# A narrow attention layer's score matmuls in two 64-row tiles, with another order of the work in a step

## What is computed

```python
# layer 1 (narrow), x: 2048 x 256, cond: 1601 x 512
q = rmsnorm(x) @ wq           # 16 heads of 16
k, v = cond @ wk, cond @ wv   # 4 heads of 16, each for 4 query heads
x = x + softmax(q @ k.T / 4) @ v @ wo
```

## Time and profile before

| | us |
|---|---|
| median of 3 runs | 4579.02 (4578.73 to 4581.03) |
| the profiled execution | 4576.37 |
| its span | 4574.6 |
| TensorE busy | 4481.5 |
| VectorE busy | 3081.8 |
| GpSimd busy | 2825.7 |
| ScalarE busy | 2308.6 |

### The profile page before, as it was taken

One profiled execution on the slowest core, in us unless ns is written; L12 is line 12 of the kernel. 1 busy time (PEld: TensorE's weight loads), 2 busy tenths in 40 slices (PEclk: granted clock), 3 DMA queues, 4 the chain that ended last, 5 costly groups with the idle time before them and its releaser, 6 DMA issues.

```text
span 4574.6 us, 56775 instructions
## 1 busy us (share of the span) xinstructions
PE 4481.5 (98%) x20609; PEld 2828.0 (62%) x20609; DVE 3081.8 (67%) x5037; ACT 2308.6 (50%) x4121; POOL 2825.7 (62%) x1365
## 2 busy tenths in 40 slices
PE   8999999999999979999999999999999999999999
PEld 7888765656566445555556566656656666666664
DVE  4221567777777678777846777777766677777776
ACT  3232554555455436666655554545555545555553
POOL 0000388889888701011136898889875888898886
PEclk9999999999999979999999999999999999999999
DMA  5474921222221021111243222222126212222220
GB/s 189 156 221 150 305 68 38 66 66 69 48 64 48 13 41 15 13 14 16 57 133 92 64 69 47 66 64 64 41 50 219 63 45 60 63 69 61 51 48 30
DMA packets 124633, 349.68 MB, mean 76 GB/s; under 512 B 28085, under 2 KB 46005, under 8 KB 113338
## 3 DMA queue, kind: packets, MB, share of 16 engines
q1 hardware_dynamic: 124352, 346.04, 28.6%
HBM read 191.31 MB, written 120.31 MB: 68 GB/s over the span
## 4 chain that ended last, share of the span: by engine, by line
PE 93%; DVE 5%; issue 1%; DMA 1%; ACT 0%; SPq 0%; DVEq 0%; ACTq 0%
PE ST L1005 14%; PE SS L986 12%; PE ST L1006 12%; PE OA L1016 12%; PE OB L1016 11%; PE ST L1150 5%; PE OA L1158 4%; PE SS L1136 3%; DVE acc L1612 2%; PE OB L1136 1%; PE SS L1025 1%; PE ST L1081 1%; PE ST L1082 1%; PE ST L1083 1%; PE SS L1052 1%
## 5 line engine op out<-in xcount | busy, mean ns | idle before, releaser
L882 POOL TENSOR_TENSOR acc<-acc,P 128x1024 f32<-128x1024 f32 x912 | 2216.9, 2463 | 298.4 <-DVE acc L1618 285.3
L1346 ACT ACTIVATE P<-ST 128x512 f32<-128x512 f32 (+1 forms) x2496 | 1464.6, 598 | 1254.2 <-PE ST L1006 1128.6
L1591 DVE TENSOR_REDUCE mpart<-SS 128x1 f32<-128x400 f32 (+1 forms) x3072 | 1629.5, 570 | 666.4 <-PE SS L986 590.7
L1005 PE MATMUL ST<-QX,KX 128*128 128x512 f32 (+1 forms) x2496 | 1022.9, 410 | 2.3 <-ACT stw L1244 2.0
L986 PE MATMUL SS<-KS,QS 68*128 68x400 f32 (+1 forms) x3072 | 977.2, 352 | 13.6 <-DMA QS<-stq 8.0
L1006 PE MATMUL ST<-QS,KS 69*128 69x512 f32 (+1 forms) x2496 | 988.4, 396 | 0.0
L986 PEld LDWEIGHTS SS<-KS,QS 68*128 68x128 f32 x3072 | 583.6, 190 | 189.8 <-DVE xacc L1642 24.9
L1005 PEld LDWEIGHTS ST<-QX,KX 128*128 128x128 f32 (+1 forms) x2496 | 463.0, 186 | 359.5 <-issue 271.2
L1016 PE MATMUL OA<-P,Vp 128*64 128x512 f32 (+1 forms) x2496 | 658.3, 606 | 0.0
L1016 PE MATMUL OB<-P,Vp 128*64 128x512 f32 (+1 forms) x2496 | 641.3, 592 | 0.0
L1445 ACT ACTIVATE PG<-ST 128x512 f32<-128x512 f32 (+1 forms) x832 | 426.5, 616 | 215.6 <-PE ST L1150 215.5
(11 more groups left out here) (247 smaller groups left out, 4457.1 us busy)
## 6 DMA issues: line engine op xcount, KB each, us to landing
q_parts<-stq SPq DMA_DIRECT2D x96, 512.0 KB, 5.2
QX<-q_parts SPq DMA_DIRECT2D x96, 512.0 KB, 11.3
KX<-k_parts SPq DMA_DIRECT2D x48, 801.0 KB, 9.4
QS<-q_parts SPq DMA_DIRECT2D x45, 512.0 KB
R<-R SPq DMA_DIRECT2D x360, 64.0 KB, 2.0
v_tiles<-sv SPq DMA_DIRECT2D x24, 832.0 KB, 5.9
Vp<-v_tiles SPq DMA_DIRECT2D x24, 832.0 KB, 7.2
k_parts<-skh SPq DMA_DIRECT2D x48, 400.5 KB, 4.8
```

Source lines behind the costliest of these rows:

```text
L882: gp.tensor_tensor(out, out, P[0:k, slot(H, t), q, :], ALU.add).then_inc(pool_a, 1)
L1005: pe.matmul(bank, KX[H % 2][:, t * 128:t * 128 + k], QX[H % 2][:, q], start=True, stop=False)
L1346: act.activation(P[0:k, slot(H, t), j, :], ST[n % 3][0:k, :], ACT.Exp, scale=SCALE).then_inc(act_p, 1)
L1591: dve.tensor_reduce(mpart[H % 2][:, i // len(KCH), c:c + 1], SS[RING_AT["s", H, i] % 3][:, 0:w], AX.X, ALU.max).then_inc(dve_ss, 1)
```

## The change

The contraction of a narrow head is cut to the three products high-high, low-high and high-low: 48 rows for a maximum (`GROWS`), 49 for a score. The operands lie twice in the partitions, at 0 and at 64 (`HALF`). Of the keys both copies are the same; of the queries the first half holds blocks 0 and 2 of 512 columns, the second blocks 1 and 3. Score j of a tile reads half j % 2, maximum i half i % 2. Nothing reads partitions that must be zero any more: three memsets go, and eight of 32 rows replace four.

A head is now thirteen steps of one key tile: three scores of the next tile, the output items or the projection where there are any, five maxima (four in one step of thirteen, seven in most of head 0), the transposed row in step 9, the fourth score, then the values of this step's tile. The ring's fourth bank is OA, and the values go to OB. The query parts take six DMAs a head instead of four, the maxima row two instead of one, the key parts 24 instead of 16 in all. VectorE and ScalarE follow the same order.

```diff
-MROW = 3 * QD + D1
+GROWS = 3 * D1
+HALF = 64
...
+GROW = KT - 4
...
+def group_units(h, t):
+
+    if t + 1 < KT:
+        return [(0, t + 1, j) for j in range(JQ)]
+    return [(1, 0, j) for j in range(JQ)] if h + 1 < HEADS else []
+
+
+def group_tiles(h, t):
+
+    if t >= GROW:
+        return 2, (part(SUNITS, t - GROW, KT) if h + 2 < HEADS else range(0))
+    if h + 1 >= HEADS:
+        return 1, range(0)
+    return 1, (part(SUNITS, t, GROW) if h == 0 else part(SUNITS, t + KT - GROW, KT))
+
+
+def group_takes_row(h, t):
+    return t == GROW and h + 1 < HEADS
+
+
+def group_takes_sums(h, t):
+    return t == 3 and h > 0
+
+
+def group_o_items(h, t):
+
+    return range(2 * t, 2 * t + 2) if h % GROUPS == 1 and h > GROUPS and t < JQ else range(0)
+
+
+def group_q_item(h, t):
+
+    return t if h % QHEADS == QHEADS - 2 and h + 2 < HEADS and t < JQ else None
...
+        GS = SS + [OA]
...
-        GS = SS + [OB]
...
+            def group_k(g):
+                for i, r in enumerate((0, 0, 1)):
+                    for half in range(2):
+                        to = HALF * half + i * D1
+                        sp.dma_start(words(KG[g][to:to + D1, :]), dKG[r, g * QD:g * QD + D1, :]).then_inc(gd_k, 16)
...
-                stack(GQ[h % 3], words(Q4hi[q, :]), words(Q4lo[q, :]), (0, 1, 0, 1), D1, gd_q[h % 3])
+                for i, src in enumerate((Q4hi, Q4lo, Q4hi)):
+                    blocks = words(src[q, :]).rearrange("d (b u c) -> d b u c", b=2, u=2)
+                    for half in range(2):
+                        to = HALF * half + i * D1
+                        sp.dma_start(words(GQ[h % 3][to:to + D1, 0:NQ // 2]).rearrange("d (b c) -> d b c", b=2),
+                                     blocks[:, :, half, :]).then_inc(gd_q[h % 3], 16)
...
-                sp.dma_start(words(GQ[h % 3][MROW:MROW + 1, :]).rearrange("o (t p) -> o t p", p=128),
-                             words(mrow[:, :])).then_inc(gd_m, 16)
+                for half in range(2):
+                    to = HALF * half + GROWS
+                    sp.dma_start(words(GQ[h % 3][to:to + 1, 0:NQ // 2]).rearrange("o (t p) -> o t p", p=128),
+                                 words(mrow[8 * half:8 * half + 8, :])).then_inc(gd_m, 16)
...
-                    gp.memset(words(k[3 * QD:4 * QD, :]), 1.0).then_inc(pool_ones, 1)
-                gp.wait_ge(pool_ones, GROUPS)
-                for q in GQ:
-                    gp.memset(words(q[:, :]), 0.0).then_inc(pool_ones, 1)
+                    for half in range(2):
+                        gp.memset(words(k[HALF * half + QD:HALF * half + 2 * QD, :]), 1.0).then_inc(pool_ones, 1)
...
             def group_s(h, i):
-                at = GRING_AT["s", h, i]
                 if i == 0:
-                    pe.wait_ge(gd_q[h % 3], 64 * (h // 3 + 1))
-                wait_group_ring(pe, at)
-                qt, (o, w) = i // len(KCH), KCH[i % len(KCH)]
-                pe.matmul(GS[at % 4][:, 0:w], GQ[h % 3][0:MROW, qt * 128:(qt + 1) * 128],
-                          KG[h % GROUPS][0:MROW, o:o + w], start=True, stop=True).then_inc(gpe_s, 1)
+                    pe.wait_ge(gd_q[h % 3], 96 * (h // 3 + 1))
+                wait_group_ring(pe, GRING_AT["s", h, i])
+                half, qt, (o, w) = i % 2, i // 2 // len(KCH), KCH[i // 2 % len(KCH)]
+                k = slice(HALF * half, HALF * half + GROWS)
+                pe.matmul(group_bank("s", h, i)[:, 0:w], GQ[h % 3][k, qt * 128:(qt + 1) * 128],
+                          KG[h % GROUPS][k, o:o + w], start=True, stop=True).then_inc(gpe_s, 1)
...
             def group_scores(h, t, j):
                 n, k = HU * h + JQ * t + j, rows_of(t)
                 if t == 0 and j == 0:
-                    pe.wait_ge(gd_m, 16 * (h + 1))
+                    pe.wait_ge(gd_m, 32 * (h + 1))
                 wait(pe, gact_p, n - 2)
-                pe.matmul(ST[n % 3][0:k, :], KG[h % GROUPS][0:MROW + 1, t * 128:t * 128 + k],
-                          GQ[h % 3][0:MROW + 1, j * 512:(j + 1) * 512], start=True, stop=True).then_inc(gpe_st, 1)
+                r = slice(HALF * (j % 2), HALF * (j % 2) + GROWS + 1)
+                pe.matmul(ST[n % 3][0:k, :], KG[h % GROUPS][r, t * 128:t * 128 + k],
+                          GQ[h % 3][r, j // 2 * 512:(j // 2 + 1) * 512], start=True, stop=True).then_inc(gpe_st, 1)
...
                 for j in range(JQ):
-                    last = pe.matmul(OA[j * QD:j * QD + QD, :], Vg[0:k, t, g * QD:g * QD + QD],
+                    last = pe.matmul(OB[j * QD:j * QD + QD, :], Vg[0:k, t, g * QD:g * QD + QD],
                                      PG[slot(h, t) * JQ + j][0:k, :], start=t == 0, stop=t == KT - 1)
...
-                for g in range(STEPS):
-                    for u, (on, t, j) in enumerate(units(h, g)):
-                        group_scores(h + on, t, j)
-                        if takes_row(h, g, u):
-                            group_transpose_max(h + 1)
-                        if group_o_item(h, g, u) is not None:
-                            group_output(h // GROUPS - 1, group_o_item(h, g, u))
-                        if group_q_item(h, g, u) is not None:
-                            group_project(h // QHEADS + 1, group_q_item(h, g, u))
-                        ahead, tiles = s_tiles(h, g, u)
-                        for i in tiles:
-                            group_s(h + ahead, i)
-                    pe.wait_ge(gact_p, HU * h + JQ * (PV[g][-1] + 1))
-                    for t in PV[g]:
-                        group_values(h, t)
-                    if takes_sums(h, g):
+                for t in range(KT):
+                    both = group_units(h, t)
+                    for on, ts, j in both[:-1]:
+                        group_scores(h + on, ts, j)
+                    for i in group_o_items(h, t):
+                        group_output(h // GROUPS - 1, i)
+                    if group_q_item(h, t) is not None:
+                        group_project(h // QHEADS + 1, group_q_item(h, t))
+                    ahead, tiles = group_tiles(h, t)
+                    for i in tiles:
+                        group_s(h + ahead, i)
+                    if group_takes_row(h, t):
+                        group_transpose_max(h + 1)
+                    for on, ts, j in both[-1:]:
+                        group_scores(h + on, ts, j)
+                    pe.wait_ge(gact_p, HU * h + JQ * (t + 1))
+                    group_values(h, t)
+                    if group_takes_sums(h, t):
                         group_sums(h - 1)
...
+                for t in range(KT):
+                    for i in group_o_items(h, t):
+                        group_add(h // GROUPS - 1, i)
+                    if group_q_item(h, t) is not None:
+                        group_lo(h // QHEADS + 1, group_q_item(h, t))
+                    ahead, tiles = group_tiles(h, t)
+                    for i in tiles:
+                        group_s_max(h + ahead, i)
+                    if group_takes_row(h, t):
+                        group_max_row(h + 1)
+                    if t == GROW - 1 and h + 1 < HEADS:
                         group_head_max(h + 1)
-                    if g == 0 and h > 0:
+                    if t == 1 and h > 0:
                         group_reciprocals(h - 1)
```

More of the change, by code:

```diff
@@ L195, in group_order @@
     for h in range(HEADS):
-        for g in range(STEPS):
-            for u in range(len(units(h, g))):
-                if takes_row(h, g, u):
-                    out.append(("m", h + 1, 0))
-                if group_o_item(h, g, u) is not None:
-                    out.append(("o", h // GROUPS - 1, group_o_item(h, g, u)))
-                if group_q_item(h, g, u) is not None:
-                    out.append(("q", h // QHEADS + 1, group_q_item(h, g, u)))
-                ahead, tiles = s_tiles(h, g, u)
-                out += [("s", h + ahead, i) for i in tiles]
-            if takes_sums(h, g):
+        for t in range(KT):
+            out += [("o", h // GROUPS - 1, i) for i in group_o_items(h, t)]
+            if group_q_item(h, t) is not None:
+                out.append(("q", h // QHEADS + 1, group_q_item(h, t)))
+            ahead, tiles = group_tiles(h, t)
+            out += [("s", h + ahead, i) for i in tiles]
+            if group_takes_row(h, t):
+                out.append(("m", h + 1, 0))
+            if group_takes_sums(h, t):
                 out.append(("z", h - 1, 0))
@@ L736, in load_gwq @@
                             .then_inc(gd_wq, 16)
-            def stack(to, hi, lo, order, height, done):
-                for i, r in enumerate(order):
-                    rows = height if i < 3 else D1
-                    src = (hi, lo)[r]
-                    sp.dma_start(words(to[i * QD:i * QD + rows, :]), src[0:rows, :]).then_inc(done, 16)
+            def group_k(g):
[3 more added lines that the diff above has]
+                        sp.dma_start(words(KG[g][to:to + D1, :]), dKG[r, g * QD:g * QD + D1, :]).then_inc(gd_k, 16)
```

(27 more changed lines are left out.)

69 lines of the change are left out of this document (26 added, 43 removed).

## The result

| | before | changed |
|---|---|---|
| median of 4 runs, us | 4580.01 (4578.73 to 4581.03) | 4667.85 (4653.05 to 4670.63) |
| ratio | | 1.0187 [1.0168, 1.0205] |
| profiled execution, its span | 4576.37, 4574.6 | 4670.63, 4669.0 |
| mean granted clock | 0.988 | 0.969 |
| heads 1 to 15 together | 619.9 | 698.7 |

A forecast was written before the change was run, and what follows sets the result against it. TensorE was taken to bound the kernel, VectorE next. Terms -2 - 1 + 7 + 2.6 + 3.3 - 1 + 0 + 1.5 = +10.4 us gave 4586.8 for the profiled execution, 4589.5 for the median; range 4550 to 4666.

The forecast's parts named there:

- the rival without overlap: Row halves do not run at once: 0.4 us more a step, +76 us, 4665 us in all; chance 14%.
- Overlap of halves, 0.01 us: TensorE matmuls in different row halves run at once, a neighbour in the other half starting 0.01 us later.
- The step of 3.00 us: One-tile step, end of values to end of values: 3.00 us, including the fifth maximum's wait for VectorE.
- Less 0.8 for the one step with four maxima (no ring wait): Ordinary head: its one step with four maxima skips the wait for a free bank, 0.8 us shorter.
- Output items, +2.3 a head: Heads 5, 9, 13: adds ahead of the first reduce and full-array switches cost 2.3 us a head, +7 in all.
- the projection head: Head 6: projection, ScalarE's copy and VectorE's subtract stand before the first reduce, +2.6 us.
- The start, +1.5: Start of the layer: +1 us for the first query copy's DMAs, +0.5 for the first maxima row.
- the waits for the maxima row, -1: Inside the layer: the maxima row leaves earlier relative to its use, so waits for it go, -1 us.
- What bounds the kernel now: Narrow layer before the change: TensorE bounds it (busy 98%, 93% of the chain), VectorE next at 31 us a head.
- The clock: +3 for head 0 in the sum, a rival at 9% for the rest: Low clock: +3 us in head 0; rival: one in seven of 208 steps falls, +48, about 4640 us, chance 9%.
- Shorter joints: Rival: half-row matmuls start output earlier and switches are cheaper, 0.15 us a step, -31 us, 4559 us; chance 22%.
- sums rule: Rival: engines' summed work, not the chain, sets the time: VectorE's 32 us a head, -115, 4465 us; chance 3%.

The follow-up runs named there:

- rows64: Changed kernel with maxima and score operands over 63 and 64 rows instead of 48 and 49 (added rows: zeros in queries, ones in keys); 4614.72 us, ratio 1.0078.
- order_only: Changed kernel's new step order with the old operands of 112 and 113 rows, nothing in halves; 4666.53 us, ratio 1.0194 to the kernel before.
- tiles_only: Kernel before in its old order and banks, with the new operands in two halves of 64 partitions; 4665.08 us, ratio 1.019.
- one_half: Changed kernel with every maxima and score matmul reading the copy in partitions 0 to 48, so none can overlap; 4891.37 us, ratio 1.0669.
- fill3: Changed kernel with each step's fourth maxima matmul issued four times instead of once, into the same bank; 4628.57 us, ratio 1.0116.
- full1: Changed kernel with one added 128-row matmul a step (400 columns), ahead of the fourth maximum in its bank; 4691.34 us, ratio 1.025.

## Why the prediction was right in sign and wrong in size

The profiled execution lost 4669.0 - 4574.6 = 94.4 us: heads 1 to 15 take 698.7 instead of 619.9, +78.8; head 0 and the start +16.0. rows64, which differs in rows alone, puts the price of the chain itself at 642.7 - 619.9 = +22.8 for heads 1 to 15 (1.5 of it for a short low stretch in head 6); the changed kernel's own undisturbed heads give +22.0. By the second figure the other 56.8 are the low clock, 15.3 of them in head 15. In head 0 the two can be told apart only in part: with rows64 it ends 8.1 us earlier. In this execution, the slowest of four, the clock's part is thus some 65 of 94 us; by the medians, where rows64 gives back 53 of 88, it is 60%.

The median lies close to another number of the prediction, the 4665 of the rival without overlap, and that is chance: the halves do overlap. order_only (4666.5) and tiles_only (4665.1) stand at the same time for two more causes. The time alone would have picked the wrong one; the heads and the clock tell them apart. The range's upper end, 4666, was set by that wrong rival as well, so that the time came so near to it is luck.

Point by point:
- **Overlap of halves, 0.01 us.** Right: score 3 and the fifth maximum start together, and one_half prices it at 4.95 us a head.
- **The step of 3.00 us.** Right (3.02), with the fifth maximum's load behind VectorE in 12 of 13 steps and the values in sets of 1.00.
- **"Less 0.8 for the one step with four maxima (no ring wait)".** Wrong: the transposed row takes the fifth place in the ring, +0.28. 0.8 + 0.28 is the whole difference between the 39.5 forecast and the 40.57 measured: some +10 over nine heads.
- **Output items, +2.3 a head.** Mis-sized: 50.19 - 46.2 = +4.0, of which 0.9 is the ordinary head's own loss; the projection head +3.8 for +2.6; head 14 no gain for -1. Head 15 at full clock, 34.03 in rows64, is near the 34.4 said.
- **The start, +1.5, and the waits for the maxima row, -1.** Near: the first exponential starts at 1668.44 instead of 1667.88, +0.6; from 1700 us to the layer's end TensorE waited once for that row before, 0.8 us, and not at all after.
- **"What bounds the kernel now": TensorE.** Incomplete: tiles_only shows ScalarE and the three score banks at the same 5.98 us a pair. That did no harm to the sum, because the new step has another chain, but it would have misjudged any lighter version in the old order.
- **The clock: +3 for head 0 in the sum, a rival at 9% for the rest.** This step failed: the sum put the low clock of heads 1 to 15 at nothing, and it cost 56.8 us there. Head 0 and the start took +16.0 where +4.8 was in the sum. The rival's arithmetic was near: it took 1.6 us a step and one step in seven; measured are 1.8 us, and 56.8 / 1.8 = 32 steps of the 195 in heads 1 to 15, one in 6. What failed was its chance. The argument against it, "every step holds values, and the last head before, at 63%, fell only once", compared shares of time in columns alone. fill3 shows that columns count, but one_half and rows64 show that rows count as well: the scores of that last head covered 113 rows, the new ones 49. The sign to look for was the opening, where 112 rows and thin columns stood at 0.50, together with the fact that the change cuts the rows to less than half.
- **Shorter joints; sums rule.** Neither: no joint came out shorter, and the ring's wait stood.

What stays open: why the low stretches begin just after a head's end (the values of a head's last tile cover 65 rows instead of 128, as at 1815.17, which fits, but no run tests it); why head 15, with identical instructions, stood at 0.58 in the changed kernel and at 1.00 in full1, whose filling had ended four steps before it; and how much a row of zeros counts against one of data. rows64 shows only that fifteen such rows are enough here.

## What to carry to other kernels

Before narrowing TensorE's operands, ask what it does to the clock: fewer rows at equal or shorter time can take back what the overlap gives. Here it was 3.8 us a head (56.8 over 15) of 4.95, and in tiles_only, where the overlap gave nothing, the kernel came out 89 us slower. Operands padded to the whole row tile of 64, with zeros on one side, cost no time in a head (40.54 us against 40.57) and held the clock but for one short stretch. Before moving work in one engine's queue, list every item of the buffer ring in order, the odd ones (a transpose) too: the fifth user of four banks waits, whoever it is. A busy share of 98% does not say that the engine is the only bound; look which other engine has the same period.

## What the runs showed of the hardware that was not expected

- Granted clock at the same columns: with 113 rows 1.00 in heads 1 to 15 (order_only), with 49 rows 0.66 over heads 1 to 11 (one_half), TensorE busy 96% and 99%. In the overlapped order, 49 rows left ten disturbed heads of fifteen; 64 rows, fifteen of them zeros on one side, left one, which lost 1.5 us.
- Matmuls in the two row halves start within 0.01 us of each other (1780.22 and 1780.22), and so do their weight loads (two of 0.18 and 0.19 us at 1778.98).
- A step costs 3.02 us at 2.4 GHz and 4.82 at 1.2 GHz: 1.6 times, not 2. A part of its chain is VectorE's: from the first maximum to the fifth it is 1.10 to 1.24 us at the full clock and 1.62 at the lower (1821.10 to 1822.72).
- A matmul of 128 rows put between tiles of 64, two records of 0.94 us together, made a step 0.41 us longer, 5.3 a head, although TensorE of the changed kernel idles 0.33 to 0.49 us at that place (full1).
